# First-layer neighbour sum of a fused four-layer graph network: three-term products from adjacency strips

## What is computed

```
h = maximum(layernorm(x), 0)
e1 = adj @ h
x = x + (h - e1 * (diag + 1)) @ W + bias
```

## Time and profile before

| | |
|---|---|
| runs (us) | 1197.0, 1202.8, 1203.67; median 1202.8 |
| profiled execution, its own time | 1198.75 us |
| its span, first to last instruction | 1196.9 us |
| mean granted TensorE clock | 0.915 |
| projection of the first layer | from about 16.5 us to 38.8 us of the span |
| gather of the first layer | 40.27 us to 92.95 us |
| next work of TensorE | 96.6 us |

### The profile page before, as it was taken

The page is one execution under the profiler, slowest core; times in us unless marked ns, Lnnn a source line. Parts: engine busy times, 40 slices in busy tenths (PEclk is TensorE's granted clock), DMA queues, the critical chain, the costliest instruction groups (busy, mean ns, idle before and its releaser), DMA issues.

```text
span 1196.9 us, 14038 instructions
## 1 busy us (share of the span) xinstructions
PE 949.0 (79%) x4873; PEld 782.5 (65%) x4873; DVE 774.0 (65%) x1297; ACT 482.1 (40%) x864; POOL 37.6 (3%) x101
## 2 busy tenths in 40 slices
PE   4998799957999779996789589978795078856874
PEld 3788688856899778995578358867442044545753
DVE  4653455453566436774589974324699999979993
ACT  4104644263232323326578612233688830211112
POOL 0000000000000000000130000001000000000000
PEclk9998899978999899997999799989998588997997
DMA  8000000000000000002124200003021000000001
GB/s 340 18 1 1 21 1 1 1 1 1 1 0 0 19 1 2 0 0 47 49 72 127 68 0 1 0 19 84 0 72 49 0 24 25 1 0 1 0 0 47
DMA packets 42895, 32.68 MB, mean 27 GB/s; under 512 B 3218, under 2 KB 40796, under 8 KB 42844
## 3 DMA queue, kind: packets, MB, share of 16 engines
q1 hardware_dynamic: 42844, 32.02, 8.8%
HBM read 30.63 MB, written 1.39 MB: 27 GB/s over the span
## 4 chain that ended last, share of the span: by engine, by line
PE 20%; DVE 13%; issue 13%; ACT 7%; ACTq 0%; DVEq 0%; POOL 0%
PE out L777 6%; ACT u_rows_a L588 3%; PE turned_ps L911 3%; PE scores L893 3%; DVE e_strip L1486 2%; PE scores L808 2%; DVE small L1269 2%; DVE run L1370 1%; DVE e_strip L1489 1%; DVE e_rows L1492 1%; PE scores L818 1%; PE turned_ps L893 1%; DVE tmp L1361 1%; PE scores L687 1%; PE turned_ps L818 1%
## 5 line engine op out<-in xcount | busy, mean ns | idle before, releaser
L588 ACT ACTIVATE u_rows_a<-e_rows,small 128x1354 f32<-128x1354 f32 x104 | 146.5, 1411 | 20.1 <-DVE small L1308 20.1
L777 PE MATMUL out<-h_rows,adj_strip 128*128 128x256 f32 x484 | 109.9, 384 | 0.0
L748 PE MATMUL out<-feat,adj_t 128*128 128x256 f32 (+1 forms) x484 | 107.5, 380 | 1.5 <-DVE x_rows L1084 1.5
L748 PEld LDWEIGHTS out<-feat,adj_t 128*128 128x128 f32 x484 | 91.4, 189 | 15.6 <-DVE x_rows L1084 1.9
L777 PEld LDWEIGHTS out<-h_rows,adj_strip 128*128 128x128 f32 x484 | 92.4, 195 | 12.2
L893 PE MATMUL scores<-feat_fb,adj_strip 128*128 128x512 f32 x154 | 73.8, 638 | 16.8 <-ACT feat_fb L603 13.3
L1314 DVE SCALAR_TENSOR_TENSOR tmp<-e_rows,small 128x1354 f32<-128x1354 f32 x52 | 84.6, 1626 | 0.0
L482 ACT ACTIVATE y_rows<-scores,small 128x1354 f32<-128x1354 f32 x22 | 30.7, 1393 | 129.8 <-DVE small L1221 129.7
L677 PE MATMUL turned_ps<-ident,tmp 128*128 128x128 f32 x132 | 30.0, 325 | 55.3 <-ACT tmp L423 38.1
L893 PEld LDWEIGHTS scores<-feat_fb,adj_strip 128*128 128x128 f32 x154 | 31.5, 207 | 56.5 <-issue 38.9
L1221 DVE TENSOR_REDUCE small<-scores 128x1354 f32 (+1 forms) x22 | 34.5, 1569 | 45.2 <-PE scores L788 45.2
(11 more groups left out here) (325 smaller groups left out, 2208.6 us busy)
## 6 DMA issues: line engine op xcount, KB each, us to landing
adj_strip<-in_adjT SPq DMA_DIRECT2D x22, 704.0 KB, 4.7
adj_t<-in_adjT SPq DMA_DIRECT2D x11, 704.0 KB, 13.2
u_weights<-in_L_gnn_U SPq DMA_DIRECT2D x8, 256.0 KB, 4.8
x_rows<-in_x SPq DMA_DIRECT2D x2, 512.0 KB, 3.9
tmp<-in_L_gnn_W_stack SPq DMA_DIRECT2D x2, 512.0 KB, 4.7
out_rows<-y_rows SPq DMA_DIRECT2D x2, 512.0 KB
tmp<-in_L_gnn_U SPq DMA_DIRECT2D x2, 256.0 KB, 2.8
x_rows<-in_x SPq DMA_DIRECT2D x1, 384.0 KB, 5.3
```

The source lines that it names most:

```text
L588: act.activation(out2[:, (k % 2) * N:(k % 2 + 1) * N], E[:, t, :], [ACT.Relu, ACT.Sign][k % 2], bias=nudged[:, t:t + 1], accum_out=[relu_s ...
L748: ins = pe.matmul(bank[:, 0:n], AT[:, j, cols(t)], features[:, j, 0:n], start=(j == 0), stop=(j == NT - 1))
L777: ins = pe.matmul(OUT[b][:, 0:D], ADJ[:, b, j, :], H[:, j, :], start=(j == 0), stop=(j == NT - 1))
```

## The change

The gather of layer one becomes a gather over strips like that of layer three.

- The projection now leaves FH (ScalarE, F32R) and FL (VectorE, one more subtraction per tile) in place of F1.
- ScalarE makes for each tile t the high strip of AT's columns, and a second copy of the block AT[:, t, :] with an accumulated sum, which is the column sum (its output goes to a scratch area). VectorE's L1107 is gone.
- VectorE makes the low strip.
- Because `hT_H` and `hT_L` occupy buffer 0, tile t uses buffer 1 - t % 2. The strip of tile 0 is made during the last turns of the projection, those of tiles 1 and 2 after it, ahead of the weight preparation of layer two, the others after that.
- TensorE does 33 F32R matmuls per tile.
- In VectorE's last loop the low strip of tile t + 3 stands ahead of the read of tile t.

```diff
-STR = {name: NT * k for k, name in enumerate(["L2a", "L2b", "A0", "A1"])}
+STR = {name: NT * k for k, name in enumerate(["L0", "L2a", "L2b", "A0", "A1"])}
...
+            def strip_l0(t, b):
+
+                wait(act, gathered, GA["L0"] + t - 1)
+                act.activation(SH[:, 1 - b, :, :], AT[:, :, cols(t)], ACT.Copy).then_inc(strip_hi, 1)
+                if not isinstance(t, int) or t >= 1:
+                    act.wait_ge(col_sums, t)
+                act.activation(expt[0], AT[:, bass.ds(t, 1), :], ACT.Copy,
+                               accum_out=colsum[:, bass.ds(t, 1)]).then_inc(col_sums, 1)
+
+            def first_strip_l0(t, r):
+                if isinstance(t, int) and t == NT - 1:
+                    act.wait_ge(ld_adj, 16 * NT)
+                    strip_l0(0, 0)
...
-            project_rows(PJ["L0"], stage_norm(PJ["L0"]), copy_part(lambda t: F1[:, bass.ds(t, 1), 0:D], 0, D, D))
+            project_rows(PJ["L0"], stage_norm(PJ["L0"]), copy_part(lambda t: FH[:, bass.ds(t, 1), 0:D], 0, D, D),
+                         before=[(3, first_strip_l0)])
             act.wait_ge(projected, PJ["L0"] + NT)
+            strip_l0(1, 1)
+            strip_l0(2, 0)
             split_w("L1", WH[:, :, 0:D + 6 + D], raw[:, :, 0:D + 6 + D])
             act.activation(WrH[:, :, :], wlr[:, :, 0:1].broadcast_to([P, KB, P]), ACT.Copy).then_inc(w_hi, 1)
+            for t in range(3, NT):
+                strip_l0(t, t % 2)
+            act.wait_ge(gathered, GA["L0"] + NT)
...
-            def gather(name, *groups):
-
-                def step(t, b):
+            def gather(name, *groups, swap=False):
+
+                def step(t, place):
+                    b = 1 - place if swap else place
                     wait(pe, strip_hi, STR[name] + t + 1)
                     wait(pe, strip_lo, STR[name] + t + 1)
                     wait(pe, gather_read, GA[name] + t - 1)
...
-            pipeline(pe, (0, gather_l0), peel=NT)
+            pipeline(pe, (0, gather("L0", one, swap=True)))
...
             def evac_l0(t, r):
                 b = r % 2
+                lo(row(FL, t), pbank[b][0][:, D:2 * D], row(FH, t))
                 link0(t, 1, dve.tensor_tensor(row(X, t), row(X, t), pbank[b][0][:, 0:D], ALU.add))
                 return dve.tensor_tensor(row(X, t), row(X, t), bcast[:, :], ALU.add)
 
-            project_rows(PJ["L0"], evac_l0)
+            def strip_rest_l0(t, b):
+                wait(dve, strip_hi, STR["L0"] + t + 1)
+                wait(dve, gathered, GA["L0"] + t - 1)
+                lo(SL[:, 1 - b, :, :], AT[:, :, cols(t)], SH[:, 1 - b, :, :]).then_inc(strip_lo, 1)
+
+            def first_rest_l0(t, r):
+                if isinstance(t, int) and t == NT - 1:
+                    dve.wait_ge(ld_adj, 16 * NT)
+                    strip_rest_l0(0, 0)
+
+            pipeline(dve, (2, turn(PJ["L0"])), (3, first_rest_l0), (4, evac(PJ["L0"], evac_l0)), peel=7, ring=RT)
+            strip_rest_l0(1, 1)
+            strip_rest_l0(2, 0)
...
-            def sum_column(t, b):
-
-                dve.tensor_reduce(one(colsum, t), AT[:, bass.ds(t, 1), :], AX.X, ALU.add).then_inc(col_sums, 1)
-
-            dve.wait_ge(ld_adj, 16 * NT)
-            pipeline(dve, (0, sum_column), (0, read(GA["L0"], read_l0)))
+            read_tile_l0 = read(GA["L0"], read_l0)
+            for t in range(NT):
+                if t + 3 < NT:
+                    strip_rest_l0(t + 3, (t + 3) % 2)
+                read_tile_l0(t, t % 2)
             dve.wait_ge(gather_read, GA["L0"] + NT)
```

More of the change, by code:

```diff
@@ L491, in _ @@
             act.wait_ge(w_lo, WPREP["L0"])
-            project_rows(PJ["L0"], stage_norm(PJ["L0"]), copy_part(lambda t: F1[:, bass.ds(t, 1), 0:D], 0, D, D))
+            project_rows(PJ["L0"], stage_norm(PJ["L0"]), copy_part(lambda t: FH[:, bass.ds(t, 1), 0:D], 0, D, D),
+                         before=[(3, first_strip_l0)])
             act.wait_ge(projected, PJ["L0"] + NT)
+            strip_l0(1, 1)
+            strip_l0(2, 0)
             split_w("L1", WH[:, :, 0:D + 6 + D], raw[:, :, 0:D + 6 + D])
             act.activation(WrH[:, :, :], wlr[:, :, 0:1].broadcast_to([P, KB, P]), ACT.Copy).then_inc(w_hi, 1)
+            for t in range(3, NT):
+                strip_l0(t, t % 2)
+            act.wait_ge(gathered, GA["L0"] + NT)
             act.activation(F2[:, :, D:D + 1], onezero[:, :, 0:1], ACT.Copy)
             act.activation(F1[:, :, D + 2:D + 3], onezero[:, :, 0:1], ACT.Copy)
-            act.wait_ge(gathered, GA["L0"] + NT)
             root("L1")
@@ L739, in step @@
                             for j in range(NT):
-                                ins = pe.matmul(OUT[b][:, c0:c0 + n], left[:, b, j, :], right[:, j, 0:n],
+                                ins = pe.matmul(OUT[place][:, c0:c0 + n], left[:, b, j, :], right[:, j, 0:n],
                                                 start=(m == 0 and j == 0), stop=(m == 2 and j == NT - 1))
@@ L750, in gather_adj @@
                 ins.then_inc(gathered, 1)
-            def gather_l0(t, b):
-                wait(pe, gather_read, GA["L0"] + t - 1)
-                gather_adj(OUT[b], F1, t, D)
             def gather_l1b(t):
```

## The result

The changed kernel takes 1249.5 us, the median of 4 runs (1246.2 to 1253.8); beside it the kernel before took 1199.9. The ratio is 1.0415, 95% interval 1.0362 to 1.0467: slower, where 1248 was forecast. The profiled execution took 1248.13 us, its span is 1246.0 us, 49.1 more than before.

A forecast was written before the change was run, and what follows sets the result against it. TensorE alone was taken to bound the gather. 28.8 us of waits plus 18 of clock, 46.8, on the profiled 1198.75 made 1245.6, or 1249.6 on the median's scale; 1248 was given, range 1228 less 2 to 1266.

The forecast's parts named there:

- Order of waits: Layer-one gather: VectorE's read of tile t waits behind tile t + 3's low strip; 8.16 us a tile, 28.8 us later.
- the rival with the clock at 2.4 GHz throughout: Gather: same waits but no clock loss in the pauses; +28.8 us, 1228 to 1232; chance 10%.
- Clock: Gather: TensorE's clock falls after nine pauses, 2.0 us for each of nine tile gathers, 18 us.
- The rival with nearly all at 1.2 GHz: Gather: same waits, 3.1 us of clock loss for each of 11 tiles; +63 us, 1262 to 1266; chance 12%.
- Tile 2: Gather: tile 2 starts at 56.4 us, after the weight preparation, ScalarE's two copies and strip 3.
- Start of the gather: End of the first projection: the gather starts at 41.7 us in place of 40.27.
- 7 subtractions of 0.42 more make 10.6, at the limit but under it: First projection: VectorE's extra subtraction fits, its 7.68 us busy in 11.52 us rising to 10.6.
- Three terms: Gather matmuls: 33 F32R matmuls take 4.02 us a tile against 4.76, saving 8.1 us over 11 if TensorE never waits.
- the measured row: Profile of layer three's strip gather: 33 F32R matmuls of 256 columns took 4.02 us, the price the prediction used.
- the count of passes: Gather matmuls: three single passes in place of true FP32's four, 3.57 us a tile, saving 13 us in all.
- The faster one: Gather: strips and reads overlap the matmuls at 4.02 us a tile; 5 us earlier, 1194 to 1198; chance 5%.
- The one without effect: Gather: with overlap, new matmuls cost what F32 ones do, 4.76 us a tile; about 1200 us; chance 2%.

The follow-up runs named there:

- filled pauses: The changed kernel with 30 F32R matmuls that nobody reads before tiles 3 to 9 and 52 before tile 2; 1229.74 us, ratio 1.0266.
- overlapped version: The changed kernel with VectorE reading tile t before the low strip of tile t + 2, weight preparation in its idle time; 1197.1 us, ratio 0.9956.
- late low part: The overlapped version with the low strip's term last, tile 0's low strip behind the evacuations, column sums 0 and 1 after their strips; 1192.24 us.
- bias on GpSimd: The late low part with GpSimd instead of VectorE adding the bias to X in the first projection; 1193.55 us, ratio 0.9945.

## Why the prediction was right

- **Order of waits.** Right, with its place and size. Forecast 8.16 us a turn at full clock; 8.20 with the clock held up. That version is also the rival with the clock at 2.4 GHz throughout, priced at 1228 to 1232 us: it took 1229.74. Pauses of 3.92 and 4.01 us where 4.1 was named. Undoing either of the two edges that close the circle brings the time back to that of before.
- **Clock.** 18 us over nine pauses were forecast. Eight of them cost it: tiles 2 to 9 took 6.15 to 6.7 us where 4.0 to 4.2 were due, some 17.7 us together. The one before tile 0 cost nothing in the profiled execution of the change. The sum fits because each of the eight cost 2.2 us rather than 2.0; that nine times 2.0 comes out the same is luck. The filled pauses move the last read by 15.7 us rather than 17.7, mostly because there tile 0 did lose 1.5 us. The rival with nearly all at 1.2 GHz fails because no tile ran wholly at that level: each lost 2.1 to 2.5 us of the 3.1 that this rival needs.
- **Tile 2.** Forecast at 56.4 us, and at 56.85 in the trace.
- **Start of the gather.** Forecast 41.7 us, was 42.34. The step that failed is "7 subtractions of 0.42 more make 10.6, at the limit but under it". The turn is a chain through three engines, not a sum on one; the projection of the change lost 1.3 us (its last tile began at 38.52 against 37.19; between 38.20 and 39.03 in the other profiled kernels with the same projection), and the extra operation alone moved the gather's start by 1.9 us. The error was 0.6 us of 47 and did not reach the forecast. The pause ahead of tile 0 was shorter for the same reason, 2.2 us in place of 3.
- **Three terms.** Forecast 4.02 us a tile, from a row where another kind of matmul stands in front; 3.94 when one tile follows another. The true F32 tile took 4.76. Of the two prices named in the prediction, the measured row was nearer than the count of passes (3.57). The gain of 0.8 us a tile is real and was simply buried.
- **Rivals with overlap.** The faster one, 5 us earlier with overlap, is what the overlapped version then did (5.0 us). Its condition, the read done before the next tile ends, was the right one to name. The one without effect fails with the tile's price, 3.94 us and not 4.76.

## What to carry to other kernels

In an in-order stream a wait holds up everything behind it, so with two buffers the release of an old result should stand ahead of the refill that waits for the newest one, or there should be a third buffer; check every pair of double buffers for such a circle before adding up loads. The sign of it here was that the busiest engine fell from all of the stretch to 62% and no other came near full (VectorE 23%, ScalarE 26%), while each was released by the next. And a pause of TensorE was paid twice, once as time and once in the clock of the work behind it: here 34 us of pauses before tiles 2 to 9, and 18 us of clock.

## What was not expected of the hardware

The same pause ahead of tile 0 does not always cost the clock. It was 2.2 us in six of the profiled kernels: tile 0 ran at full speed in the change and lost 1.5 us in the other five. After 1.79 us (late low part) it lost too, while the kernel before with the extra subtraction kept 1.00 through its whole gather after a pause of the same 1.79 us:

```profile
42.18:94.86 52.68, 52.53 (x242) 45.67 (x242) 28.87 (x44) 1.59 (x4) 0.00 (x0) 1.00 0.00 0
```

After 1.33 us (bias on GpSimd), and after the 1.47 us of the earlier trace rows, it did not lose either. What decides between equal pauses was not tested.
